# Four-group transformer kernel: order of the first two expert mixtures and of the causal attention

## The reference, cut to what matters

```python
x = x + 0.5 * _L0_ffn_ref(_layernorm(x), ...)    # first mixture
x = x + _L0_attn_ref(_layernorm(x), ...)
x = x + 0.5 * _L0_ffn_ref(_layernorm(x), ...)    # second mixture
...
x = x + _L1_attn_ref(_layernorm(x), ...)         # the causal stage
```

## Time and profile before

| what | value |
|---|---|
| median of 3 runs | 2413.13 us (2411.46 to 2414.87) |
| the profiled execution: its time, its span | 2413.39 us, 2411.2 us |
| granted TensorE clock, mean | 0.948 |
| PE busy, weight loads busy | 2187.4 us (91%), 1352.0 us (56%) |
| DVE, ACT, POOL busy | 1512.3 (63%), 1047.5 (43%), 105.7 us (4%) |
| chain that ended last, by engine | PE 82%, DVE 12%, ACT 3%, issue 3%, DMA 1% |

### The profile page before, as it was taken

One profiled execution on the slowest core, in us unless ns is written; L12 is line 12 of the kernel. 1 busy time (PEld: TensorE's weight loads), 2 busy tenths in 40 slices (PEclk: granted clock), 3 DMA queues, 4 the chain that ended last, 5 costly groups with the idle time before them and its releaser, 6 DMA issues.

```text
span 2411.2 us, 39296 instructions
## 1 busy us (share of the span) xinstructions
PE 2187.4 (91%) x13616; PEld 1352.0 (56%) x13616; DVE 1512.3 (63%) x4341; ACT 1047.5 (43%) x1798; POOL 105.7 (4%) x246
## 2 busy tenths in 40 slices
PE   6589999998899989999999997999999599998698
PEld 3423333335577756656656565777676367775476
DVE  6798888855443456666666665444455735777776
ACT  3137766662343345545455453433433133342133
POOL 3021111110000000000000000000000000000000
PEclk8679999996899999999999998999999699999899
DMA  6010000000000000000000000000100000000000
GB/s 210 29 55 27 25 25 25 25 14 14 1 1 1 1 1 1 1 0 0 0 0 0 0 1 1 1 1 1 55 1 1 0 1 1 1 1 1 1 1 18
DMA packets 22536, 32.76 MB, mean 14 GB/s; under 512 B 5470, under 2 KB 13931, under 8 KB 21644
## 3 DMA queue, kind: packets, MB, share of 16 engines
q1 hardware_dynamic: 21708, 30.59, 3.8%
q10 hardware_dynamic: 576, 0.26, 0.1%
q0 software_dynamic: 128, 0.26, 0.1%
HBM read 25.47 MB, written 5.24 MB: 13 GB/s over the span
## 4 chain that ended last, share of the span: by engine, by line
PE 82%; DVE 12%; ACT 3%; issue 3%; DMA 1%; ACTq 0%; POOL 0%; DVEq 0%; POOLq 0%
PE ps L409 19%; PE ps L394 18%; PE ps L605 6%; PE ps L639 5%; PE ps L2039 5%; PE ps L2007 5%; PE ps L2024 5%; PE ps L622 3%; PE ps L589 3%; DVE x L820 1%; ACT arena L737 1%; PE ps L611 1%; PE ps L335 1%; DVE stat L130 1%; DVE arena L802 1%
## 5 line engine op out<-in xcount | busy, mean ns | idle before, releaser
L409 PEld LDWEIGHTS ps<-l_w,arena 128*128 128x128 f32 x4096 | 544.4, 194 | 262.5 <-issue 249.0
L409 PE MATMUL ps<-l_w,arena 128*128 128x128 f32 x4096 | 547.6, 277 | 12.4 <-DVE x L496 10.9
L394 PE MATMUL ps<-xnT,l_w 128*128 128x512 f32 x1024 | 537.3, 608 | 3.0 <-ACT xnT L265 3.0
L496 DVE SCALAR_TENSOR_TENSOR x<-ps,comb,x 128x128 f32<-128x128 f32 x768 | 216.3, 345 | 377.9 <-PE ps L409 376.1
L452 ACT ACTIVATE arena<-ps,l_b 128x512 f32<-128x512 f32 x384 | 263.7, 687 | 409.9 <-PE ps L394 409.8
L2222 DVE TENSOR_REDUCE arena<-ps 128x1 f32<-128x512 f32 x512 | 325.5, 685 | 34.8 <-PE ps L2007 34.8
L2150 ACT ACTIVATE arena<-ps 128x1024 f32<-128x1024 f32 x256 | 252.6, 1023 | 125.4 <-PE ps L2024 124.7
L802 DVE TENSOR_REDUCE arena<-ps 128x1 f32<-128x128 f32 (+7 forms) x256 | 179.1, 752 | 76.0 <-PE ps L611 74.7
L737 ACT ACTIVATE arena<-ps,arena 128x128 f32<-128x128 f32 (+7 forms) x256 | 187.0, 745 | 72.4 <-DVE arena L802 72.4
L2007 PE MATMUL ps<-arena 128*128 128x512 bf16 x512 | 186.6, 395 | 7.7 <-DVE arena L2222 5.5
L745 ACT ACTIVATE arena<-ps 128x512 f32<-128x512 f32 (+1 forms) x192 | 85.4, 490 | 211.5 <-PE ps L622 211.3
(11 more groups left out here) (361 smaller groups left out, 1988.9 us busy)
## 6 DMA issues: line engine op xcount, KB each, us to landing
arena<-s_parts_q SPq DMA_DIRECT2D x96, 48.0 KB
arena<-s_parts_k SPq DMA_DIRECT2D x96, 48.0 KB
l_w<-in_l_w SPq DMA_DIRECT2D x2, 2048.0 KB, 14.2
l_w<-in_l_w SPq DMA_DIRECT2D x4, 1024.0 KB, 12.7
s_parts_q<-arena SPq DMA_DIRECT2D x2, 768.0 KB, 4.5
s_parts_k<-arena SPq DMA_DIRECT2D x2, 768.0 KB, 5.3
arena<-arena SPq DMA_DIRECT2D x96, 2.0 KB
x<-in_x SPq DMA_DIRECT2D x4, 256.0 KB, 5.1
```

Source lines behind the costliest of these rows:

```text
L394: pe.matmul(k.ps[:, n % 2, :], w.w1[:, e, f * P:(f + 1) * P], k.xnT[:, g * GW:(g + 1) * GW], start=True, stop=True).then_inc(s.hidden_mm.s ...
L409: ins = pe.matmul(k.ps[:, 2 + e % 4, j * P:(j + 1) * P], w.h[:, n % 2, j * P:(j + 1) * P], w.w2[:, e, f, :], start=(f == 0 and j == 0), st ...
L496: ins = dve.scalar_tensor_tensor(k.x[:, t, :], k.ps[:, 2 + e % 4, j * P:(j + 1) * P], k.comb[:, t, e:e + 1], k.x[:, t, :], ALU.mult, ALU.add)
```

## The change

**Causal stage.** The projections move between the two halves of the transposes; values and output products move behind the second half, so that they stand next to the following scores. k's projections wait for the copy of q instead of the addition to x; the output products wait for the copy of k or v out of bank 7. ScalarE always copies transposed probabilities before the next exp and copies q before o. VectorE copies k and v before the transposed probabilities and adds last.

**Mixtures.** The second mixture now takes u0, then the chosen rows, then u1 to u3. The choice comes after all experts' halves are gated; the sigmoid comes after the silus, with a one-element exp behind it. The shared output bias is no longer put in by L1485; it is kept as 128 equal rows (`b3r`) and POOL adds it to all of x by one tensor_tensor of 128x2048, once the normalised rows are read. `delta` is copied by ScalarE. `shared(0)` comes ahead of `scatter(1, 1)`, so the two halves of x are complete one after the other. `keep_busy` issues bf16 products of 128x128 with 128x512 zeros into bank 3, which nobody reads: 10 ahead of the transposes of `ze`, 30 at the end of each of the two mixtures.

```diff
@@ -666,41 +666,45 @@
                 if u == 2:
                     values(f, b, (0, 1), first=begin)
                 turn(f, u, 0, begin)
+                if not end:
+                    if u == 0:
+                        pe.wait_ge(s.kv_out, 4 * f + 4)
+                        if b == 1:
+                            pe.wait_ge(s.slices, 2 * p + 4)
+                        project("q", 0, p + b, 1 - b, 7)
+                    if u == 1:
+                        pe.wait_ge(s.q_out, 2 * f + 3)
+                        project("k", 0, p + b, 1 - b, 7)
+                    if u == 2:
+                        pe.wait_ge(s.kv_out, 4 * f + 5)
+                        if not begin:
+                            pe.wait_ge(s.y_used, 4 * f - 1)
+                        project("q", 1, p + b, 1 - b, 7)
+                    if u == 3:
+                        pe.wait_ge(s.q_out, 2 * f + 4)
+                        project("k", 1, p + b, 1 - b, 7)
+                    if u == 4:
+                        pe.wait_ge(s.y_used, 4 * f + 1)
+                        project("v", 0, p + b, 1 - b, 7)
+                    if u == 5:
+                        pe.wait_ge(s.kv_out, 4 * f + 7)
+                        project("v", 1, p + b, 1 - b, 7)
+                turn(f, u, 1, begin)
                 if u == 0 and not begin:
                     values(f - 1, 1 - b, (6, 7))
                 if u == 1 and not begin:
-                    if not end:
-                        pe.wait_ge(s.q_out, 2 * f + 3)
+                    pe.wait_ge(s.kv_out, 4 * f + (4 if end else 5))
                     output(2 * f - 1, before)
                 if u == 2:
                     values(f, b, (2, 3), first=begin)
                 if u == 3:
-                    if not end:
-                        pe.wait_ge(s.q_out, 2 * f + 4)
+                    if end:
+                        pe.wait_ge(s.y_used, 4 * f - 1)
+                    else:
+                        pe.wait_ge(s.kv_out, 4 * f + 6)
                     output(2 * f, p)
                 if u == 4:
                     values(f, b, (4, 5))
-                if u == 0 and not end:
-                    pe.wait_ge(s.kv_out, 4 * f + 4)
-                    if b == 1:
-                        pe.wait_ge(s.slices, 2 * p + 4)
-                    project("q", 0, p + b, 1 - b, 7)
-                if u == 2 and not end:
-                    pe.wait_ge(s.kv_out, 4 * f + 5)
-                    project("q", 1, p + b, 1 - b, 7)
-                if u in (4, 5) and not end:
-                    pe.wait_ge(s.kv_out, 4 * f + (6 if u == 4 else 7))
-                    project("v", u - 4, p + b, 1 - b, 7)
-                turn(f, u, 1, begin)
-                if u == 1 and not end:
-                    if begin:
-                        pe.wait_ge(s.q_out, 2 * f + 3)
-                    else:
-                        pe.wait_ge(s.y_used, 4 * f - 1)
-                    project("k", 0, p + b, 1 - b, 7)
-                if u == 3 and not end:
-                    pe.wait_ge(s.y_used, 4 * f + 1)
-                    project("k", 1, p + b, 1 - b, 7)
...
-                if u != 2:
-                    weights_out(f, u)
+                weights_out(f, u)
                 if u < U - 1:
                     exp(f, b, u + 1, begin)
                 elif not end:
                     exp(f + 1, 1 - b, 0)
-                if u == 2:
-                    weights_out(f, u)
+                if u in (0, 2) and not end:
+                    q_copy(f + 1, 1 - b, u // 2, 7)
                 if u == 0 and not begin:
                     o_copy(2 * f - 1)
                 if u == 2:
                     o_copy(2 * f)
-                if u in (0, 2) and not end:
...
                     negmax(f, u + 1)
                 elif not end:
                     negmax(f + 1, 0)
+                if u in (4, 5) and not end:
+                    kv_copy("v", f + 1, 1 - b, u - 4, 7)
+                if u in (1, 3) and not end:
+                    kv_copy("k", f + 1, 1 - b, u // 2, 7)
+                weights_out(f, u)
                 if u == 1 and not begin:
                     add(f * 2 - 1, (1 - b) * TB + GT)
                 if u == 3:
                     add(f * 2, b * TB)
-                if u in (4, 5) and not end:
-                    kv_copy("v", f + 1, 1 - b, u - 4, 7)
-                weights_out(f, u)
-                if u in (1, 3) and not end:
-                    kv_copy("k", f + 1, 1 - b, u // 2, 7)
...
         else:
-            self.order = ("u0", "u1", "u2", "u3", "m", "e0", "e1", "e2", "e3")
-            self.bank = dict(u0=5, u1=4, u2=3, u3=2, m=4, e0=0, e1=1, e2=2, e3=3)
-            self.ahead, self.m_bank = ("u0", "u1", "u2", "u3", "e0", "e1"), 7
+            self.order = ("u0", "m", "e0", "e1", "e2", "e3", "u1", "u2", "u3")
+            self.bank = dict(u0=5, m=4, e0=0, e1=1, e2=2, e3=3, u1=4, u2=7, u3=6)
+            self.ahead, self.m_bank = ("u0", "m", "e0", "e1", "e2", "e3"), 6
...
-    pool.tensor_scalar(w.lnh[:, :], w.ln[:, 1:2], 0.5, None, ALU.mult)
+    pool.tensor_scalar(w.lnh[:, :], w.ln[:, 1:2].broadcast_to([P, P]), 0.5, None, ALU.mult)
...
+        pool.wait_ge(w.prepared, 1)
+    pool.wait_ge(s.rows_v.sem, s.rows_v.at(NG))
+    pool.wait_ge(s.rows_a.sem, s.rows_a.at(NG))
+    pool.tensor_tensor(k.x[:, :, :], k.x[:, :, :], w.b3r[:, :].unsqueeze(1).broadcast_to([P, NT, D]), ALU.add)\
+        .then_inc(s.biased.sem, 1)
...
-        pe.wait_ge(s.mul.sem, s.mul.at(s.at("m")))
+        pe.wait_ge(s.sig.sem, s.sig.at(1))
         hidden("u1")
...
         turn_rows(2)
+        pe.wait_ge(s.ready.sem, s.ready.at(2))
+        turn_slots()
+        for what in ("m", "e0", "e1", "e2", "e3"):
+            hidden(what)
+        turn_rows(3)
+        pe.wait_ge(s.sig.sem, s.sig.at(1))
         hidden("u1")
-        turn_rows(3)
+        pe.wait_ge(s.ready.sem, s.ready.at(3))
         hidden("u2")
+        pe.wait_ge(s.ready.sem, s.ready.at(4))
         hidden("u3")
-        turn_slots()
-        pe.wait_ge(s.mul.sem, s.mul.at(s.at("u1")))
-        hidden("m")
-        hidden("e0")
-        hidden("e1")
-        pe.wait_ge(s.mul.sem, s.mul.at(s.at("u3")))
-        hidden("e2")
-        hidden("e3")
 
     pe.wait_ge(s.mul.sem, s.mul.at(s.at("e3")))
+    keep_busy(pe, k, 3, 10)
...
-    pe.wait_ge(s.mul.sem, s.mul.at(9))
-    for bank in range(4):
-        pe.matmul(k.ps[:, 4 + bank, :], k.ones[0:1, :], w.b3c[0:1, :].unsqueeze(1).broadcast_to([1, GT, P]),
-                  start=True, stop=False, skip_group_check=True)
...
-                          s.delta[:, m, :], start=False, stop=False, skip_group_check=True)
+                          s.delta[:, m, :], start=(j == 0 and m == 0), stop=False, skip_group_check=True)
...
+    pe.wait_ge(s.mul.sem, s.mul.at(9))
     pe.wait_ge(s.e_out.sem, s.e_out.at(1))
     scatter(0, 0)
     scatter(0, 1)
     turn_hidden(0)
     turn_hidden(1)
     scatter(1, 0)
+    shared(0)
     scatter(1, 1)
-    shared(0)
     shared(1)
+    keep_busy(pe, k, 3, 30)
+
+
+def keep_busy(pe, k, bank, n):
+
+    for i in range(n):
+        pe.matmul(k.ps[:, bank, :], k.ident_bf[:, :], k.zeros[:, :], start=True, stop=True)
...
-        act.wait_ge(s.hidden.sem, s.hidden.at(s.at("m")))
+        act.wait_ge(s.mul.sem, s.mul.at(s.at("m")))
         act.activation(s.rt[:, 1, :], k.ps[:, s.bank["m"], 2 * P:2 * P + 18], ACT.Sigmoid).then_inc(s.sig.sem, 1)
...
     rows(0)
     if s.first:
         slots_out()
-        rows(1)
-        rows(2)
-        rows(3)
-        sigmoid()
-        for what in ("m", "e0", "e1", "e2", "e3"):
-            silu(what)
-        rows_out(0)
-        rows_out(1)
-        exps()
-        silu("u0")
-        rows_out(2)
-        silu("u1")
-        rows_out(3)
-        silu("u2")
-        silu("u3")
-    else:
-        rows(1)
-        rows(2)
-        rows(3)
+    for g in range(1, NG):
+        rows(g)
+    if not s.first:
         rows_out(0)
         rows_out(1)
         silu("u0")
         rows_out(2)
-        silu("u1")
+        slots_out()
+    for what in ("m", "e0", "e1", "e2", "e3"):
+        silu(what)
+    sigmoid()
+    act.activation(s.mix[0:1, 7, :], k.ones[0:1, 0:s.MT], ACT.Exp)
+    if s.first:
+        rows_out(0)
+        rows_out(1)
+    exps()
+    if s.first:
+        silu("u0")
+        rows_out(2)
+    else:
         rows_out(3)
-        silu("u2")
-        silu("u3")
-        slots_out()
-        sigmoid()
-        for what in ("m", "e0", "e1", "e2", "e3"):
-            silu(what)
-        exps()
+    silu("u1")
+    if s.first:
+        rows_out(3)
+    silu("u2")
+    silu("u3")
...
+    act.wait_ge(s.e_mm.sem, s.e_mm.at(1))
+    act.activation(s.delta[:, :, :].rearrange("p m d -> p (m d)"), k.ps[:, 3, 0:s.M], ACT.Copy).then_inc(s.e_out.sem, 1)
...
-    if s.first:
-        ins = gated("m")
-        for what in ("e0", "e1"):
-            ins = gated(what)
-        choose()
-        for what in ("e2", "e3"):
-            ins = gated(what)
```

(50 more changed lines are left out.)

## The result

The changed kernel takes 2387.99 us (median of four runs, 2380.76 to 2389.79); the kernel before, on the same chip, 2414.00 (2411.46 to 2415.21). The ratio is 0.9888, 95% interval 0.9873 to 0.9903: about 26 us or 1.1% faster. The forecast was 2374, range 2361 to 2393. The profiled execution took 2386.22 us (span 2384.4) against 2413.39 before, 27.2 less.

What follows compares the result with a forecast made beforehand. It took TensorE's instructions and hand-overs to bound the causal stage and a serial chain the mixtures. From 2413.39 us, -15 causal, -9 first mixture, -13.5 second and -1.5 behind, sum -39, gave 2374 us, range 2361 to 2393.

Steps and rivals of the forecast that it cites:

- Rival C: Causal stage: the waits that come in cancel the gain there; -24 us in all, 2389 us, chance 0.13.
- Rival B: Mixtures: fillers don't hold the clock, both experts' parts stay at 0.50; -25 us in all, 2388 us, chance 0.18.
- L589 wait: Causal stage: k's projection no longer waits for VectorE's addition; 1.1 us per image and about 0.4 for refilling go.
- changes of tiling: Causal stage: 24 per image and head pair become 17; at 0.14 us each, 1.0 us saved.
- wait of the values: Causal stage, unit 2: values (0,1) wait for VectorE's addition to x, so TensorE stands for 0.85 us.
- wait for k's copy in unit 3: Causal stage: the output products wait for VectorE's copy of k, 0.55 us in this unit.
- First mixture: Experts and shared groups of the first mixture: last statistics at 75.4 instead of 84.7, -9 us.
- Their cycle is 2.14 us: First mixture, shared groups: taken to follow each other by 2.14 us, the last ending at 53.0 instead of 50.4.
- Second mixture: The second mixture's chain: end at 597.6 where the last statistics ended at 611.1 before, -13.5 us.
- POOL's hold: Second mixture: POOL's bias addition holds up VectorE's chain normalising the chosen rows, which ends 4.4 us later.
- The fillers: Mixtures: ten filler products ahead of the experts' transposes cost 2.2 us; the experts' products are taken at full clock.
- After each mixture: Behind the mixtures: thirty fillers block nothing, and the mixture behind the second starts warm; -1.5 us.

Runs made afterwards that it cites:

- E11: Changed kernel with the value products of causal units 0 and 4 back between the two halves of the transposes: 2393.96 us, ratio 0.9894.
- E9: The changed kernel itself, run once more as a control: 2388.68 us, ratio 0.9893.
- E6: Changed kernel with filler products added in the waits ahead of the shared groups, ten in the first mixture and eight in the second: 2381.72 us.
- E7: Changed kernel without the one-row bias products of shared groups u1 to u3 in both mixtures, their bias left out of the result: 2373.32 us.
- E5: Changed kernel with POOL's addition of the output bias also waiting for VectorE's chosen rows: 2378.96 us, ratio 0.9854.
- E4: Changed kernel without the ten fillers ahead of the experts' transposes in both mixtures: 2384.73 us, ratio 0.9880.
- E12: Changed kernel, causal output banks swapped, no fillers before experts' transposes, POOL's addition behind chosen rows, fillers before shared groups, 128-row bias products for u0 to u3: 2347.40 us.

## Why the prediction was right or wrong

- **Direction, size.** Faster, as forecast; 26 us instead of 39. Rival C's sum (2389) and B's (2388) are near the measured time, but neither mechanism is what happened. That the time lies in the stated range is luck in part: the range was drawn wide enough to take in B and C, and the half clock where it fell was in neither.
- **Causal, what goes.** The L589 wait went as forecast. The changes of tiling were counted rightly (the timelines have 24, 17, and 19 in E11) and mis-sized: 0.20 us (E11), not 0.14; seven are 1.4 per round instead of 1.0.
- **Causal, what comes in.** The wait of the values was 1.21 us, forecast 0.85. The two terms that were off are in the timeline: the values were ready 1.38 after the addition's start, not 1.55, and VectorE's release takes 0.24, not 0.03. The wait for k's copy in unit 3 was 0.71 (forecast 0.55), in unit 1 none (0.05). So 1.4 + 1.5 - 1.21 - 0.71 = 0.98 per round, with the forecast's own 1.5 for the L589 waits (1.1 of it in the list, 0.4 assumed); the period fell by 0.93. Forecast 1.05.
- **Causal, the rest.** 11.6 instead of 15: 0.1 per round, 1.6 at the start, where half clock from 864.56 to 867.98 met the second unit's scores (13.74 us from the first unit's scores to the third's, 12.1 in E9 and in the kernel before), and the rest less gain in the last rounds, which have parts only. Nothing in the forecast provided for the second; E9 shows that it does not come in every execution.
- **First mixture: the failing step.** "Their cycle is 2.14 us" for the shared groups. It was 4.00 from the half clock that began at 41.95, 0.4 us behind an idle time of 2.04. I had looked for the clock only where the experts' products stand, and had it fall, in the rival, from 55.5; in the new order the idle time (TensorE waits for ScalarE's two table loads) stands ahead of the groups with their one-row products. E6 and E7 suggest that the two together bring the fall to this place; they do not prove it. The steps after that stand: with the clock at 1.0 there (E5) the stage took 42.7 us from the m products to the last statistics (33.43 to 76.15), the forecast 42.1 (33.3 to 75.4), the changed kernel 49.5, the kernel before 51.8. By that measure the first mixture gained 2.3 us, not 4.2.
- **Second mixture.** POOL's hold of 4.4 us and everything up to the scaled rows within 0.3 us; then the same failing step: u3's products end at 575.4 at half clock where the forecast had, corrected for the start, 571.2. The fillers at half clock took 3.5 us. 8.1 instead of 13.5.
- **The fillers.** The forecast gave them a price of 2.2 and left open whether they hold the clock. E4: no. In the first mixture the clock was back 2.2 us after their start, at the same distance from its fall as without them, and the experts' products and the scatter behind ran at full clock in E4 too. Rival B had the place wrong.
- **After each mixture.** Thirty fillers blocked nothing (first: they end at 84.0, the next product is at 88.64). The stage behind the second mixture ran at 1.0 from 608.57 but for 3.4 us from 622.22 (before, 0.50 from 608.44 to 622.1 and 3.4 us from 635.75), 0.7 instead of 1.5 us gained.

**What stays open.** It is open why one execution of unchanged code (E5) had no half clock over these groups while seven had. It is open, too, whether the idle time, the one-row products or the position in time brings the clock down (in E12 it fell over the scatter without one-row products), and whether the 128 rows or the gain in spacing kept the clock up over the groups of E12; one profile of it is one observation.

## What to carry to other kernels

When an order of work is changed, draw the clock and the idle gaps of the new order for every stretch in front of the one that is meant to gain, not only for that one; the same products at half clock can eat what the shorter chain gives. When a consumer waits for a bank that another engine drains in halves, look which half it needs: exchanging two banks gave back 1.2 us in each of 15 rounds. And ask of each filler whether the clock's return moves when it is taken out, and of each window at full clock what stands right behind it: in two profiles the half clock had only moved on to the scatter.

## What the runs showed of the hardware

- A change of tiling between neighbouring products cost 0.20 us (E11). Two hand-overs between one-row and 128-row products cost 0.38 us more per group than with 128-row products alone (2.14 against 1.76).
- TensorE 100% busy in the records (17.07 of 17.07 us, 10.24 of 10.24) was at 1.2 GHz, with one-row bias products as somewhat over a third of its time; in E12, with 128-row products in their place and fillers ahead, it was at 2.4 GHz over the same groups and at 1.2 GHz for 3.4 us over the scatter behind. The Trainium skill, TensorE: Matmul & The Clock Gate, Part 1, sets the clock by how busy TensorE has been of late. The busy share of a window in the trace does not tell the clock here: it was at 1.2 GHz at 100% (17.07 of 17.07 us) and at 2.4 GHz at 94% (20.07 of 21.44).
- A POOL addition of two SBUF inputs held a two-column tensor_scalar of VectorE with one SBUF input (4.38 us instead of 0.17), but neither its statistics nor its operations that read PSUM.
- VectorE's release of a waiting TensorE product took 0.24 us from the end of the addition (1018.85 to 1019.09 in the changed kernel).
